# An attention and mixture-of-experts layer on one core: the order and the engines of its first stage changed

## The chip, the core and the metric

The kernel runs on one core of a Trainium2 chip. The metric is the device time of one execution, in microseconds; lower is better. The engines are named PE (TensorE, matrix products), ACT (ScalarE), DVE (VectorE), POOL (GpSimd) and SP (SyncE, which here only issues transfers). ACT and POOL issue transfers as well.

## The reference

Eight batches of 512 tokens with 256 channels. Each batch is normalised, and both an attention with 16 heads and an expert layer read the normalised rows; the output is the input plus both.

```python
xn = _layernorm(x)                                   # (8, 512, 256)
latent = xn @ w_kv_down                              # 256 -> 128
k, v = split(latent @ w_kv_up)                       # 16 heads of 64
q = xn @ w_q
att = softmax(where(causal, q @ k.T / 8, -inf))
y = (att @ v).reshape(..., 1024) @ w_out
logits = xn @ gate_w.T + lb_bias                     # 8 experts, the best 2 of each token
out = x + y + routed_experts(xn, logits) + shared_expert(xn)
```

## The kernel before

Products that need more than one pass's precision are made from a high and a low part: ACT copies a value to the high part (L861), DVE or POOL subtracts it from the value to get the low part (L1138 on DVE, L1350, L1355 and L1403 on POOL), and PE adds three products, high by high, high by low and low by high (L670 to L672). This holds for the weights (`split_w`: parts d, kA, qA, vA for the first heads, and qB, kB, vB for the later ones), the transposed rows, the latent, the queries and the keys.

One list of ticks (`work_order`) sets the order on all five engines. Each engine walks the list and picks what is its own, some of it with a lag in ticks (`LAG`). Engines run apart and meet at semaphores; inside an engine nothing overtakes. The list is built from pairs of heads: pair P stands at 4 P units, and other work is placed at a number of units (`at(u, ...)`, constants in `AT`). Before unit 0 lies the first batch's head: `norm_stats`, `norm_scale`, `norm_rows` (the transposes, L784), `latent`, `query` 0 and `key` 0.

For a pair, PE makes the scores (L693), DVE adds the mask and takes the row maximum (L1242; called the maxima below), ACT exponentiates (L925), PE transposes (L703), ACT or DVE copies the transposed rows (L861, L1248), and PE makes the products with the values (`attend`, L712). The scores of a pair wait for the low part of its query (L1138) and of its key (L1224), both on DVE.

The normalisation of batches 1 to 7 runs beside the first pairs, since routing to experts needs the logits of all tokens. For batch b: `norm_stats` on DVE (L1148, L1154), the reciprocal deviation on POOL (L1342, L1347), `norm_scale` on DVE (L1159), `norm_rows` on PE, ACT and DVE, `gate_logits` and `gate_columns`. Rows live in one of two buffers (`x_in(b)`): x of batch b + 2 can be loaded only after the scaled rows of batch b were stored to `xn_scratch` (L564) and transposed (L568 is the load). The transposed rows go to `xs_scratch` (L571), and the weights of the experts are split one by one (`split_moe`: load L559, ACT, POOL L1355, store L591) and loaded again into `wr` once all rows of batch 7 have been stored (L625). All these transfers are issued by SP, in the order of the ticks.

## Time and profile before

| | |
|---|---|
| time of 3 runs, median (lowest to highest) | 992.47 us (992.27 to 993.35) |
| the profiled execution's own time | 992.81 us |
| its span in the trace | 991.0 us |
| PE busy | 947.4 us (96%) |
| DVE, ACT, POOL busy | 699.7 us (71%), 650.9 us (66%), 350.6 us (35%) |
| mean granted clock of PE | 0.988 |

The span runs from the first to the last instruction. A busy share is an average over stages; the stage that the change touches is the first 125 us of 991. The granted clock is a share of full speed: 1.00 is 2.4 GHz and 0.50 is 1.2 GHz.

### The profile page before, as it was taken

The page shows a single profiled execution, that of the slowest core. Times are in us where ns is not written, and L with a number is a line of the kernel's source. Part 1 is how long each engine was busy: PE and PEld are TensorE (multiplying, and loading weights), DVE is VectorE, ACT ScalarE, POOL GpSimd, SP SyncE. Part 2 cuts the span into 40 slices and gives each one's busy share as a digit, 9 for nine tenths or more (in the row PEclk, how much of TensorE's full clock was granted, in tenths as well). Part 3 has the DMA queues.
Part 4 walks back from the last instruction along what each step waited for, and adds up shares of the span by engine and source line. Part 5 has one row for each costly group of instructions (what it writes and reads, how often), then busy time and mean ns, then how long its engine had stood idle before and what let it go on. Part 6 is the DMA issues. An engine that isn't in the chain of part 4 may idle for free.

```text
span 991.0 us, 20111 instructions
## 1 busy us (share of the span) xinstructions
PE 947.4 (96%) x7136; PEld 758.3 (77%) x7136; DVE 699.7 (71%) x2000; ACT 650.9 (66%) x1801; POOL 350.6 (35%) x349
## 2 busy tenths in 40 slices
PE   5679998889999999999999999999999999999998
PEld 4456776667788787888888888888878778777776
DVE  5779699786766657666575656666566786888884
ACT  3747667566767667676666766677666775677772
POOL 0231113453243253532434433444221444444441
PEclk9799999899999999999999999999999999999999
DMA  6486423553234435455354552547434442533421
GB/s 194 160 313 245 163 101 120 170 192 97 86 105 162 140 113 169 123 186 181 95 173 117 203 181 86 165 134 182 160 116 127 154 128 76 179 107 106 123 86 43
DMA packets 66002, 142.76 MB, mean 144 GB/s; under 512 B 7856, under 2 KB 40880, under 8 KB 64112
## 3 DMA queue, kind: packets, MB, share of 16 engines
q1 hardware_dynamic: 52896, 91.77, 28.3%
q0 software_dynamic: 12432, 49.29, 16.1%
q8 instruction: 57, 0.93, 0.4%
q10 hardware_dynamic: 576, 0.42, 0.1%
q14 instruction: 41, 0.34, 0.1%
HBM read 104.76 MB, written 36.70 MB: 143 GB/s over the span
## 4 chain that ended last, share of the span: by engine, by line
PE 84%; issue 7%; DVE 5%; POOL 2%; DMA 1%; ACT 1%; SPq 0%; DVEq 0%; POOLq 0%
PE PS L670 15%; PE PS L671 14%; PE PS L672 14%; PE PS L712 13%; PE PS L703 13%; PE PS L693 12%; PE PS L820 2%; POOL hh L1355 1%; DVE acc L986 1%; DVE pp L1242 1%; DMA xs<-xs_scratch 1%; PE PS L718 1%; POOL rstd L1347 1%; DMA xr<-in_w_moe 0%; DVE acc L1159 0%
## 5 line engine op out<-in xcount | busy, mean ns | idle before, releaser
L925 ACT ACTIVATE pp<-pp,nmax 128x128 f32<-128x128 f32 (+3 forms) x512 | 280.7, 551 | 97.4 <-DVE nmax L1242 97.4
L1242 DVE CUSTOM_DVE_ANT_0 pp<-PS,maskw 128x128 f32<-128x128 f32 (+3 forms) x512 | 215.2, 483 | 4.8 <-PE PS L693 3.4
L1403 POOL TENSOR_TENSOR yy<-yf,yy 128x512 fp32r<-128x512 f32 x63 | 82.4, 1307 | 278.9 <-ACT yy L861 278.5
L703 PE MATMUL PS<-ident,pp 128*128 128x128 f32 x1280 | 165.3, 276 | 0.1
L693 PE MATMUL PS<-qk 64*128 64x256 f32 (+2 forms) x1536 | 146.8, 337 | 15.3 <-issue 8.4
L703 PEld LDWEIGHTS PS<-ident,pp 128*128 128x128 f32 x1280 | 141.1, 140 | 14.9 <-issue 9.9
L712 PE MATMUL PS<-pt,vv 128*64 128x512 f32 (+3 forms) x1024 | 152.0, 439 | 0.0
L693 PEld LDWEIGHTS PS<-qk 64*128 64x128 f32 x1536 | 114.5, 191 | 31.0 <-issue 17.1
L712 PEld LDWEIGHTS PS<-pt,vv 128*64 128x64 f32 x1024 | 67.9, 136 | 90.3 <-issue 74.1
L861 ACT ACTIVATE pt<-PS 128x384 f32<-128x384 f32 (+1 forms) x215 | 108.5, 512 | 3.1 <-PE PS L703 3.1
L1248 DVE COPY pt<-PS 128x384 f32<-128x384 f32 x169 | 99.1, 591 | 12.7 <-PE PS L703 12.7
L1397 POOL TENSOR_TENSOR hh<-hf,hh 128x256 fp32r<-128x256 f32 (+1 forms) x55 | 49.6, 901 | 147.1 <-ACT hh L861 146.3
L925 ACT ACTIVATION_READ_ACCUMULATOR pp<-pp,nmax 128x1 f32 x512 | 96.4, 188 | 0.0
L1379 POOL DMA_INDIRECT xr<-xn_scratch,lg x78 | 74.5, 955 | 33.5 <-issue 13.8
L670 PE MATMUL PS<-woH,yy 128*128 128x256 f32 x256 | 78.5, 307 | 3.4 <-DVE acc L1209 1.9
L861 ACT ACTIVATE yy<-yf 128x512 fp32r<-128x512 f32 (+1 forms) x65 | 40.3, 622 | 52.1 <-DVE yf L1260 46.4
L672 PE MATMUL PS<-woH,yy 128*128 128x256 f32 x256 | 72.8, 284 | 0.0
L671 PE MATMUL PS<-woL,yy 128*128 128x256 f32 x256 | 72.8, 284 | 0.0
L1260 DVE TENSOR_TENSOR yf<-PS,rb 128x512 f32<-128x512 f32 x63 | 43.4, 689 | 41.2 <-PE PS L712 41.2
L1224 DVE SCALAR_TENSOR_TENSOR qk<-PS,qk 128x512 fp32r<-128x512 f32 x64 | 44.0, 688 | 35.3 <-ACT qk L910 35.0
L1390 POOL DMA_INDIRECT xg<-y_scratch,lg x64 | 61.8, 966 | 18.1 <-issue 14.7
L1138 DVE TENSOR_TENSOR qk<-PS,qk 128x512 fp32r<-128x512 f32 x64 | 44.1, 688 | 28.2 <-ACT qk L861 27.4
(166 smaller groups left out, 2051.7 us busy)
## 6 DMA issues: line engine op xcount, KB each, us to landing
rb<-rr_scratch SPq DMA_DIRECT2D x128, 128.0 KB
wr<-wm_scratch SPq DMA_DIRECT2D x16, 768.0 KB, 5.4
y_scratch<-acc SPq DMA_DIRECT2D x39, 256.0 KB
acc<-in_x SPq DMA_DIRECT2D x15, 512.0 KB, 5.4
wm_scratch<-hh SPq DMA_DIRECT2D x10, 768.0 KB, 4.0
xs_scratch<-wr SPq DMA_DIRECT2D x7, 1024.0 KB, 5.3
xs<-xs_scratch SPq DMA_DIRECT2D x7, 1024.0 KB, 4.7
xn_scratch<-acc SPq DMA_DIRECT2D x8, 512.0 KB, 3.1
```

Of the source, the lines that this page charges most:

```text
L670: e.matmul(o, aH, bH, start=first and i == 0, stop=False)
L671: e.matmul(o, aH, bL, start=False, stop=False)
L672: done = e.matmul(o, aL, bH, start=False, stop=last and i == len(pairs) - 1)
L693: done = e.matmul(bank(kind, i, 2 * j + h)[:, at:at + n], a[r, q], m[r, 0:n], start=first is True, stop=first is None)
L703: done = e.transpose(o, pp[:, i % 4, P_AT[t] + 128 * kt:P_AT[t] + 128 * kt + 128], ident[:, :])
L712: done = e.matmul(g[64 * h:64 * h + 64, 128 * kt:512], vv[:, i // 2 % 2, kt, n % 4, :], pt[:, n % 4, PT_AT[kt]:PT_AT[kt] + 512 - 128 * kt] ...
L861: return e.activation(o, i, ACT.Copy)
L925: e.activation(scores, scores, ACT.Exp, scale=-1.0, bias=nmax[:, b, t:t + 1], accum_out=rs[:, i % 4, 2 * t + h:2 * t + h + 1]).then_inc(a_ ...
L1242: e.tensor_tensor_reduce(pp[:, b, P_AT[t]:P_AT[t] + n], g[:, at:at + n], maskw[:, 512 - n:512], -1.0, 3e38, ALU.add, ALU.min, accum_out=nm ...
L1248: e.tensor_copy(pt_part(i, j), bank(kind, i, j)[:, 0:512 if j == 0 else 384]).then_inc(v_pt, 1)
L1379: e.indirect_dma_start(xr[:, 2 * (b % 2) + t, :], None, xn_d[:, :], bass.IndirectOffsetOnAxis(token_of[:, n:n + 1], 0)).then_inc(d_xr[b % ...
L1403: e.tensor_tensor(yy[:, i % 2, 1, :], yf[:, :], f32(yy[:, i % 2, 0, :]), ALU.subtract).then_inc(g_yl, 1)
```

## The change

TensorE multiplies a tile of ones by itself 15 times before the first transposes and 5 times before the first latent, into a bank that is overwritten. The first batch's x is issued half by SP and half by ACT, and transfers that are needed later are issued later. `query` 1 is placed before the scores of pair 0, `key` 1 and `query` 2 soon after them. The low parts of qB, kB and vB are computed by POOL and no longer by DVE, and they signal `g_wlo` where they signalled `v_wlo`. The mask's first 384 columns, which are zero, are set by POOL, and 128 columns are loaded. `norm_stats`, `norm_scale` and `norm_rows` of batches 1 to 7 are placed 0.6 to 0.8 units later, and the first two `split_moe` 4.3 units later.

```diff
@@ constants
-AT = {"query": (0.0, 0.9), "key": (2.3, 2.0), "value": (1.1, 2.1), "out_part": (3.2, 0.2), "stats": -3.7,
-      "scale": -2.2, "rows": -1.6, "first": 54.0, "last": 176.0, "split": -1.3, "experts": 23.0, "shared0": 17.0,
+AT = {"query": (0.0, 0.9), "key": (2.3, 2.0), "value": (1.1, 2.1), "out_part": (3.2, 0.2), "stats": -3.1,
+      "scale": -1.6, "rows": -0.8, "first": 54.0, "last": 176.0, "split": 3.0, "experts": 23.0, "shared0": 17.0,
@@ def work_order
-        at(4 * (P - 2) + AT["query"][P % 2] if P else -9, "query", P)
-        at(4 * (P - 2) + AT["key"][P % 2] if P else -8, "key", P)
+        at(4 * (P - 2) + AT["query"][P % 2] if P > 2 else (-9, -6, -1.5)[P], "query", P)
+        at(4 * (P - 2) + AT["key"][P % 2] if P > 1 else (-8, -3.5)[P], "key", P)
-    for u, name in ((-8.5, "vA"), (-1.3, "qB"), (-1.2, "kB"), (-1.1, "vB")):
+    for u, name in ((-6.5, "qB"), (-1.2, "kB"), (-1.1, "vB")):
     put("split_w", "kA")
-    put("split_w", "qA")
     for c in range(2):
         put("norm_rows", 0, c)
         tick()
+    put("split_w", "qA")
+    put("split_w", "vA")
@@ def sync_program
-            for t in range(4):
+            for t in range(2):
                 e.dma_start(x_in(0)[:, t, :], x[0, 128 * t:128 * t + 128, :]).then_inc(d_x0[t], 16)
-            e.dma_start(ident[:, :], consts[:, 0:128]).then_inc(d_ident, 16)
             for name in WEIGHT_PARTS:
                 e.dma_start(raw_w[name][0], raw_w[name][1]).then_inc(d_wraw[name], 16)
                 if name == "vA":
-                    e.dma_start(x_in(1), rows128(x[1])).then_inc(d_xin[1], 16)
+                    e.dma_start(hf[:, 0, 0:128], consts[:, 1184:1312]).then_inc(d_mask, 16)
+            e.dma_start(x_in(1), rows128(x[1])).then_inc(d_xin[1], 16)
+            e.dma_start(lb[:, :], lb_bias).then_inc(d_lb, 16)
+            e.dma_start(kc[:, :], consts[:, 384:672]).then_inc(d_kc, 16)
@@ def tensor_program
+            def warm(n):
+                for _ in range(n):
+                    e.matmul(bank("latent", 0, 0)[:, 0:128], ones[:, :], ones[:, :], start=True, stop=True)
+            w.wait_ge(g_cst, 1)
+            warm(15)
...
                 elif kind == "latent":
+                    if not i:
+                        warm(5)
@@ def scalar_program
-            e.dma_start(gw[:, :, :], gate_w).then_inc(d_gw, 16)
-            e.dma_start(hf[:, 0, :], consts[:, 800:1312]).then_inc(d_mask, 16)
-            e.dma_start(lb[:, :], lb_bias).then_inc(d_lb, 16)
-            e.dma_start(kc[:, :], consts[:, 384:672]).then_inc(d_kc, 16)
+            for t in range(2, 4):
+                e.dma_start(x_in(0)[:, t, :], x[0, 128 * t:128 * t + 128, :]).then_inc(d_x0[t], 16)
+            e.dma_start(ident[:, :], consts[:, 0:128]).then_inc(d_ident, 16)
+            e.dma_start(gw[:, :, :], gate_w).then_inc(d_gw, 16)
@@ def vector_program
-                elif kind == "split_w" and lag == 0:
+                elif kind == "split_w" and lag == 0 and i not in LATE_PARTS:
@@ def gpsimd_program
+            e.memset(maskw[:, 0:384], 0.0).then_inc(g_cst, 1)
+                elif kind == "split_w" and lag == 0 and i in LATE_PARTS:
+                    raw, _, oH, oL = raw_w[i]
+                    w.wait_ge(a_whi, whi_at[i])
+                    e.tensor_tensor(oL, raw, f32(oH), ALU.subtract).then_inc(g_wlo, 1)
```

`LATE_PARTS` is qB, kB and vB. All waits on their low parts (three on PE, one on DVE, two on SP) now ask for `g_wlo`.

Three places of the order carry the prediction. The first is DVE's list between the maxima of pair 0 and those of pair 1, before the change; `qk<-PS,qk` at L1138 is the low part of query 1, and at L1224 that of key 1.

```order
L1138 TENSOR_TENSOR qk<-PS,qk 128x512 [waits s_a_q]
L1148 BN_STATS st<-acc 128x6 [waits s_d_xin1,s_v_mv]
L1148 BN_STATS st<-acc 128x6 x3
L1154 BN_AGGR mv<-st 128x2 [waits s_v_st,s_g_ve,s_v_xn]
L1154 BN_AGGR mv<-st 128x2 [waits s_v_st] x3
L1138 TENSOR_TENSOR wqL<-pp,wqH 128x2x768 [waits s_a_whi]
L1138 TENSOR_TENSOR wkL<-acc,wkH 128x768 [waits s_a_whi]
L1138 TENSOR_TENSOR wvL<-xr,wvH 128x768 [waits s_a_whi]
L1224 SCALAR_TENSOR_TENSOR qk<-PS,qk 128x512 [waits s_a_k]
L1159 TENSOR_SCALAR acc<-acc,mv,rstd 128x256 [waits s_g_rstd]
L1159 TENSOR_SCALAR acc<-acc,mv,rstd 128x256 x3
L1253 RECIPROCAL rr<-rs 128x8 [waits s_a_exp]
```

The same place of DVE's list in the changed kernel, from the last of the maxima of pair 0 to the first of pair 1 (lines are those of the changed file); the query here is number 2.

```order
L1241 SCALAR_TENSOR_TENSOR qk<-PS,qk 128x512 [waits s_a_k]
L1155 TENSOR_TENSOR qk<-PS,qk 128x512 [waits s_a_q]
L1165 BN_STATS st<-acc 128x6 [waits s_d_xin1,s_v_mv]
L1165 BN_STATS st<-acc 128x6 x3
L1171 BN_AGGR mv<-st 128x2 [waits s_v_st,s_g_ve,s_v_xn]
L1171 BN_AGGR mv<-st 128x2 [waits s_v_st] x3
L1271 RECIPROCAL rr<-rs 128x8 [waits s_a_exp]
L1260 ISA pp,nmax<-PS,maskw 128x128 [waits s_g_wlo,s_p_S]
```

The low part of key 1 now comes first and nothing of the weights is left on DVE; the low part of query 2 stands ahead of the statistics, and the scaling of batch 1 (L1159 before) is gone from here. It stands behind the maxima of pair 1, in front of the next part of DVE's list:

```order
L1176 TENSOR_SCALAR acc<-acc,mv,rstd 128x256 [waits s_g_rstd]
L1176 TENSOR_SCALAR acc<-acc,mv,rstd 128x256 x3
L1165 BN_STATS st<-acc 128x6 [waits s_d_xin0,s_v_mv]
L1165 BN_STATS st<-acc 128x6 x3
L1171 BN_AGGR mv<-st 128x2 [waits s_v_st,s_g_ve,s_v_xn]
L1171 BN_AGGR mv<-st 128x2 [waits s_v_st] x3
L1266 COPY pt<-PS 128x384 [waits s_p_T]
L1155 TENSOR_TENSOR wr<-PS,wr 128x512 [waits s_a_xth] x2
L1196 TENSOR_TENSOR lg<-PS,lb 128x32 [waits s_d_lb,s_p_lgc]
L1176 TENSOR_SCALAR acc<-acc,mv,rstd 128x256 [waits s_g_rstd]
L1176 TENSOR_SCALAR acc<-acc,mv,rstd 128x256 x3
L1165 BN_STATS st<-acc 128x6 [waits s_d_xin1,s_v_mv]
```

Both scalings (of batches 1 and 2) are followed by statistics, and the last row, the statistics of batch 3, waits for a load of x that SP issues. SP's list around that load, before the change, from the store of batch 1's rows (L564) to the load (L568):

```order
L564 DMA xn_scratch<-acc 128x4x256 [waits s_v_xn]
L591 DMA wm_scratch<-hh 128x1536 [waits s_g_wm]
L559 DMA xr<-in_w_moe 128x768
L659 DMA acc<-in_w_out 128x1024
L568 DMA acc<-in_x 128x4x256 [waits s_d_xn1,s_p_xt]
```

And in the changed kernel, from the same store (L572) to the same load (L576):

```order
L572 DMA xn_scratch<-acc 128x4x256 [waits s_v_xn]
L604 DMA rr_scratch<-rrT 4x2x128 [waits s_a_rb]
L579 DMA xs_scratch<-wr 128x2048 [waits s_v_xtl]
L612 DMA rb<-rr_scratch 64x512 [waits s_v_wlo,s_d_rr]
L612 DMA rb<-rr_scratch 64x512
L576 DMA acc<-in_x 128x4x256 [waits s_d_xn1,s_p_xt]
```

The expert weights and `w_out` are no longer between the two; the reciprocals of pair 0 and the transposed rows of batch 1 (1 MB, waiting for `v_xtl`, DVE's low parts) are.

## Rows read from the trace of the kernel before

**Rows 1.** The page: busy time, share of the span and instructions of PE.

```profile
PE 947.4 (96%) x7136; PEld 758.3 (77%) x7136; DVE 699.7 (71%) x2000; ACT 650.9 (66%) x1801; POOL 350.6 (35%) x349
```

**Rows 2.** Windows: stretch, length, busy time of each engine, granted clock, DMA share, GB/s.

```profile
25.00:50.00 25.00, 15.96 (x94) 11.88 (x95) 18.89 (x61) 18.23 (x43) 7.46 (x9) 0.80 0.51 166
50.00:90.00 40.00, 34.19 (x242) 23.60 (x241) 33.97 (x109) 22.84 (x61) 12.30 (x13) 1.00 0.84 295
90.00:110.00 20.00, 19.84 (x149) 14.40 (x150) 13.63 (x49) 13.02 (x39) 1.29 (x1) 1.00 0.58 217
```

**Rows 3.** Timeline of PE: start, duration, instruction, idle before and its releaser.

```profile
12.14 0.79 PE L670 MATMUL PS<-xs,wdH 128*128 128x512 f32 x1 [1.41 <-DVE xs L1138]
...
19.68 2.20 PE L693 MATMUL PS<-qk 64*128 64x256 f32 x24 [0.34 <-DVE qk L1224]
...
33.26 3.89 PE L693 MATMUL PS<-qk 64*128 64x256 f32 x24 [8.40 <-issue]
```

**Rows 4.** Window 29 to 39 us, columns as in rows 2.

```profile
29.00:39.00 10.00, 5.74 (x29) 4.67 (x30) 8.96 (x25) 4.10 (x12) 1.83 (x1) 0.50 0.31 94
```

**Rows 5.** Timeline of DVE, 5 to 86 us.

```profile
5.26 0.94 DVE L1148 BATCH_NORM_STATS2 st<-acc 128x6 f32<-128x256 f32 x2 [0.42 <-DMA acc<-in_x]
...
10.02 0.69 DVE L1138 TENSOR_TENSOR wqL<-pp,wqH 128x512 fp32r<-128x512 f32 x1 [0.34 <-ACT wqH L861]
...
20.77 0.29 DVE L1242 CUSTOM_DVE_ANT_0 pp<-PS,maskw 128x128 f32<-128x128 f32 x1 [1.23 <-issue]
...
29.06 1.76 DVE L1138 TENSOR_TENSOR wqL<-pp,wqH 128x1536 fp32r<-128x1536 f32 x1 [2.65 <-ACT wqH L861]
...
32.48 0.68 DVE L1224 SCALAR_TENSOR_TENSOR qk<-PS,qk 128x512 fp32r<-128x512 f32 x1
...
34.91 0.29 DVE L1242 CUSTOM_DVE_ANT_0 pp<-PS,maskw 128x128 f32<-128x128 f32 x1 [0.35 <-PE PS L693]
...
46.89 1.41 DVE L1148 BATCH_NORM_STATS2 st<-acc 128x6 f32<-128x256 f32 x4 [0.43 <-DMA acc<-in_x]
...
50.86 2.65 DVE L1159 TENSOR_SCALAR acc<-acc,mv,rstd 128x256 f32<-128x256 f32 x4
...
59.97 1.40 DVE L1148 BATCH_NORM_STATS2 st<-acc 128x6 f32<-128x256 f32 x4 [2.55 <-DMA acc<-in_x]
...
85.02 1.41 DVE L1148 BATCH_NORM_STATS2 st<-acc 128x6 f32<-128x256 f32 x4
```

**Rows 6.** Timeline of ACT, the split of qB.

```profile
27.56 1.48 ACT L861 ACTIVATE wqH<-pp 128x1536 fp32r<-128x1536 f32 x1
```

**Rows 7.** Timeline of SP's issues, batches 1 and 3: store, then next load.

```profile
34.48 0.37 SPq L564 DMA_DIRECT2D xn_scratch<-acc  x1
...
40.58 0.38 SPq L568 DMA_DIRECT2D acc<-in_x  x1
...
55.16 0.51 SPq L564 DMA_DIRECT2D xn_scratch<-acc  x1
...
61.31 0.38 SPq L568 DMA_DIRECT2D acc<-in_x  x1
```

**Rows 8.** The loads of x at L568 before 110 us, from issue to landing.

```profile
DMA to landing us min/median/max: 3.9/5.3/7.6
```

**Rows 9.** Timeline of POOL, a split of 768 columns and one of 1024.

```profile
36.62 1.83 POOL L1355 TENSOR_TENSOR hh<-xr,hh 128x768 fp32r<-128x768 f32 x1 [8.75 <-ACT hh L861]
...
49.99 2.40 POOL L1350 TENSOR_TENSOR woL<-acc,woH 128x1024 fp32r<-128x1024 f32 x1
```

**Rows 10.** Timeline of PE: the scores of pair 4, and the first expert product.

```profile
89.96 2.21 PE L693 MATMUL PS<-qk 64*128 64x256 f32 x24
...
113.23 0.47 PE L670 MATMUL PS<-xs,wr 128*128 128x512 f32 x1
```

**Rows 11.** Transfers issued from 90 to 115 us: size, median time from issue to landing.

```profile
wr<-wm_scratch SPq DMA_DIRECT2D x3, 768.0 KB, 6.4
xs_scratch<-wr SPq DMA_DIRECT2D x2, 1024.0 KB, 4.6
```

More of the change, by code:

```diff
@@ L40 @@
 WEIGHT_PARTS = ("d", "kA", "qA", "vA", "qB", "kB", "vB")
+LATE_PARTS = WEIGHT_PARTS[4:]
 BUSY_HEADS = range(7, 22)
@@ L341, in attention_moe_kernel @@
             new_sem("v_" + n) for n in ("max", "pt", "rr", "y", "yl", "bt", "sg", "h", "add", "fx"))
-        g_cst, g_ve, g_rstd, g_wm, g_wo, g_yl, g_hl, g_sel = (
-            new_sem("g_" + n) for n in ("cst", "ve", "rstd", "wm", "wo", "yl", "hl", "sel"))
+        g_cst, g_wlo, g_ve, g_rstd, g_wm, g_wo, g_yl, g_hl, g_sel = (
+            new_sem("g_" + n) for n in ("cst", "wlo", "ve", "rstd", "wm", "wo", "yl", "hl", "sel"))
         block = ctx.enter_context(nc.Block())
@@ L369, in attention_moe_kernel, with low_weights @@
         whi_at = {n: i + 1 for i, n in enumerate(WEIGHT_PARTS)}
+        def low_weights(name):
+            return (g_wlo, whi_at[name] - 4) if name in LATE_PARTS else (v_wlo, whi_at[name])
         group_of = {k: item[-1] for k, item in enumerate(items)}
@@ L557, in moe_load @@
                 else:
-                    w.wait_ge(v_wlo, whi_at["vB"])
+                    w.wait_ge(*low_weights("vB"))
                 e.dma_start(xr_w, w_moe[SPLIT_ORDER[q]]).then_inc(d_wmraw, 16)
@@ L657, in sync_program @@
                     else:
-                        w.wait_ge(v_wlo, whi_at["kB"])
+                        w.wait_ge(*low_weights("kB"))
                     e.dma_start(acc[:, 0, :, :].rearrange("p t n -> p (t n)"), out_w(i)[0]).then_inc(d_wout, 16)
@@ L722, in tensor_program @@
                     w.wait_ge(*xs_ready(b))
-                    w.wait_ge(v_wlo, whi_at["qA" if p < 2 else "qB"])
+                    w.wait_ge(*low_weights("qA" if p < 2 else "qB"))
                     w.wait_ge(*free)
@@ L730, in tensor_program @@
                     w.wait_ge(v_lat, b + 1)
-                    w.wait_ge(v_wlo, whi_at["kA" if p < 2 else "kB"])
+                    w.wait_ge(*low_weights("kA" if p < 2 else "kB"))
                     w.wait_ge(*free)
@@ L737, in tensor_program @@
                     w.wait_ge(v_lat, b + 1)
-                    w.wait_ge(v_wlo, whi_at["vB" if g4 else "vA"])
+                    w.wait_ge(*low_weights("vB" if g4 else "vA"))
                     w.wait_ge(*free)
@@ L787, in tensor_program @@
                     w.wait_ge(v_xtl, 2 * i + 2)
-                    w.wait_ge(v_cst, 2)
+                    w.wait_ge(v_cst, 3)
                     w.wait_ge(*free)
@@ L1165, in vector_program @@
                     if i == "vA":
+                        w.wait_ge(d_mask, 16)
+                        e.tensor_copy(maskw[:, 384:512], hf[:, 0, 0:128]).then_inc(v_cst, 1)
                         w.wait_ge(d_gw, 16)
                         e.tensor_copy(gwH[:, :, :], gw[:, :, :]).then_inc(v_cst, 1)
-                        w.wait_ge(v_cst, 1)
+                        w.wait_ge(v_cst, 2)
                         low(gwL[:, :, :], gw[:, :, :], gwH[:, :, :]).then_inc(v_cst, 1)
-                        w.wait_ge(d_mask, 16)
-                        e.tensor_copy(maskw[:, :], hf[:, 0, :]).then_inc(v_cst, 1)
                 elif kind == "norm_rows" and lag == 1:
@@ L1226, in vector_program @@
                 elif kind == "scores" and lag == LAG["max"]:
-                    w.wait_ge(v_cst, 3)
+                    w.wait_ge(v_cst, 1)
+                    w.wait_ge(g_cst, 3)
                     for h in range(2):
@@ L1240, in vector_program @@
                             else:
-                                w.wait_ge(v_wlo, whi_at["qB" if i else "kA"])
+                                w.wait_ge(*low_weights("qB" if i else "kA"))
                             e.tensor_tensor_reduce(pp[:, b, P_AT[t]:P_AT[t] + n], g[:, at:at + n], maskw[:, 512 - n:512], -1.0, 3e38, ALU.add, ALU.min,
```

## The prediction, made before the changed kernel was run

> **What bounds the kernel now.** I read the page first: PE is busy 947.4 us of 991.0 [rows 1], so 43.6 us of idle time is all that an edit without less PE work can win. The windows say where it lies [rows 2]: from 25 to 50 us PE is busy 15.96 of 25 us, from 50 to 90 us 34.19 of 40, from 90 to 110 us 19.84 of 20. From 90 us on PE has no room, and its work there is the same before and after the change. So the question is how much earlier PE reaches the place in its list that it now reaches at 89.96 us, the scores of pair 4 [rows 10]; up to there both kernels have done the same pieces except the warming products.
>
> Up to 90 us PE waits for others. DVE is busy 33.97 of 40 us between 50 and 90, and the transfers 0.84 [rows 2]. The timeline of PE shows the largest wait: 8.40 us before the scores of pair 1 at 33.26, which then take 3.89 us, where the same 24 products took 2.20 at 19.68 [rows 3]. The granted clock is 0.50 from 29 to 39 us [rows 4], the lower of the two levels; PE had stood still since 25. DVE's timeline says what was waited for: the low part of key 1 starts at 32.48, queued behind the splits of qB, kB and vB from 29.06, and those waited 2.65 us for ACT [rows 5]. Later DVE itself waits for x: 0.43 us at 46.89, 2.55 us at 59.97 [rows 5].
>
> **The change part by part.** I follow the chain to four marks.
>
> *To the maxima of pair 0.* DVE's statistics of the last two x tiles start at 5.26 [rows 5]. Two of four tiles now go by ACT's queue, ahead of the constants that used to be there. I take 1.0 us for it; bounds 0 and 1.4 (four statistics of some 0.45 in a row cannot end much before 5). wqL (0.69 us at 10.02) no longer stands before the low parts of x [rows 5]: 0.7. The latent thus starts near 12.14 - 1.7 = 10.4 [rows 3]. Fifteen warming products are 128 columns wide in two passes, which I estimate at 0.43 us each at the lower level (as many column passes as half a latent product, at two cycles a column), so they end by 7.4 at the latest, when the transposes start; the five others fill the gap before the latent (1.1 us at the higher level, 2.1 at the lower). If the clock is then at 2.4 GHz, the latent and query 0 save up to 1.6 us: by the ratio of the two scores, 3.89 to 2.20 [rows 3], on the 3.6 us that they take before the clock rises now. Scores 0 could start at 16 to 17 instead of 19.68, with query 1 (1.4 us) already done. But DVE has the low part of query 1 ahead of the maxima, and ACT makes its high part only after the split of qB, 1.48 us [rows 6]: value copy to 15.7, split to 17.2, query copy 0.6, low part 0.7. Maxima of pair 0 start at 18.4, against 20.77 [rows 5]: 2.4 earlier.
>
> *To the maxima of pair 1.* They take 3.4 us; key 1's low part follows (0.68) and PE starts scores 1 at 22.5 instead of 33.26 [rows 3]. The 8.40 us wait is gone and the 1.7 us of slow clock too, as no idle time is left that is near the one before 29 us. What is late next is DVE: it waits for query 2's high part on ACT. ACT's list up to the split of qB reaches 27.56, which is 6.8 us after the maxima began at 20.77 [rows 5, 6]; the new list up to query 2 has the same pieces, so 25.2. Then 0.7 low part, 1.75 statistics: the maxima of pair 1 start at 27.6 instead of 34.91 [rows 5]: 7.3 earlier.
>
> *To the load of x for batch 3.* The scaling of batch 1 now stands behind these maxima, and its deviation is computed on POOL behind three splits. POOL takes 1.83 us for 768 columns [rows 9]: qB's 1536 from 17.2 to 20.9, kB and vB to 29.7, then 1.4 for the deviation: 31.1. The maxima end at 31.0. The scaling ends at 32.5, its store is issued there instead of at 34.48 [rows 7]: only 2.0 earlier. Five of the 7.3 us are handed back. The load of batch 3 was issued 6.1 us after the store and landed 6.3 us later (40.58, then DVE at 46.89) [rows 5, 7]. Now SP must first issue the 1 MB of transposed rows, which wait for statistics 2, a copy and two low parts on DVE (32.5 + 3.8 = 36.3), and two broadcasts: load at 38.0, landed after 5.3 to 6.3 [rows 7, 8], 43.8. DVE stands idle from 37.9 on, some 6 us. Batch 3's statistics: 3.1 earlier, and the low part of key 2 with the scores of pair 2 behind them.
>
> *To the scores of pair 4.* From 43.8: statistics and key 2 2.4, copies and low parts 2.6, maxima of pair 2 3.4, scaling 1.4: batch 3's store at 53.6 (before: 55.16). Its load comes 6.15 later, as 61.31 came after 55.16 [rows 7], and lands 5.3 later [rows 8]: 65.1. Statistics 1.7, 2.5 of copies, maxima 3.4, low part 0.6, scaling 1.4: 74.7; store to load 4.0, landing 5.3: batch 7's statistics at 84.0 instead of 85.02 [rows 5]. Key 4's low part now follows them at once (2.4 us), and PE's transposes of batch 6 are done by then: scores of pair 4 at 86.4 instead of 89.96 [rows 10], 3.6 earlier. Bounds: 84.1 if x is never late (PE's own list), 88.5 if each of three loads lands 0.7 us later.
>
> *Behind it.* The rows of batch 7 are transposed ten ticks' worth of work later, in front of the first expert product (23.3 us after the scores of pair 4, at 113.23) [rows 10]. Their store can be issued 13.7 after the scores, lands in 4.6, and then the weights load, 5.0 to 6.4 [rows 11]: 23.3 to 24.7. I take a new wait of 0.5 us.
>
> Costs of nothing: the mask and the memset (POOL idle, 0.3 us of DVE saved); the later splits of the first experts (ACT 0.84, POOL 1.83 [rows 9]; they leave the crowded stretch, are due only for the weight loads behind the norms, and cost nothing as long as they end by then); gate weights early.
>
> Sum: 3.6 - 0.5 = 3.1 us off 992.81, the profiled execution's own time: 989.7. The median of the runs is 0.34 lower, so 989.4.
>
> Two rules of the Trainium skill bear on this. The DMA page (DMA: Bandwidth & Descriptors, Issuing engines are not separate DMA queues) says that transfers from several engines run on the same 16 DMA engines, so that two queues save only issue time; by it the x term would be the time of two issues, about 0.9 us, and no trace here shows x issued that way yet. The GPSIMD page (GPSIMD Engine Reference, Key points) says that GpSimd shares its SBUF interfaces with VectorE, which speaks against moving the splits to POOL. The trace agrees in one place: four scalings beside POOL's split at 49.99 took 2.65 us [rows 5, 9], about twice what they take alone. By that rule, if it hit one or two groups of four on the chain to the load of x, the sum would be 1.3 to 2.6 us worse; without it, it stays 3.1.
>
> **The rivals.**
> A: x is not what limits. If the loads land in 3.9 [rows 8] and stores clear quickly, DVE's idle 6 us near 40 and the waits behind it shrink, and the 7.3 us of the second mark mostly stays. For it: DVE loses 3.7 us of work. Against it: the same load already ended two waits of DVE [rows 5]. Gain 5 to 7.5, time 986.0.
> B: all is handed back. The chain store, load, statistics, maxima, scaling takes 38.1 us for two rounds now (46.89 to 85.02 [rows 5]) and 40.2 in my sum, since the maxima stand inside it; if each round loses 0.5 to 1.5 us more, batch 7's statistics stay at 85 to 86.5 and scores 4 at 88.5 to 89: gain 0.4 to 1, time 991.9.
> C, slower: PE waits for the first expert weights. The store of batch 7's rows and the weight load need 4.6 + 6.4 us behind a start 13.7 to 15 us after scores 4; with landings as long as 7.6 [rows 8] that is 29 us against 23.3, a wait of up to 5.7. It decides the sign once that wait exceeds the gain at scores 4. Time 994.6.
> D: the warming does not raise the clock, or it falls back before the latent. Then PE enters the latent at the lower level and the five products delay it by 1 us: the first mark is 1 to 2.6 us worse, of which ACT's split hides about half. Time 990.6. The forecast of the clock rests on PE having worked at the lower level from 12.14 and from 33.26 for less than 6 us each time before its products were fast [rows 3, 4]; 15 products at that level last 6.4.
>
> **How the numbers follow.** Likeliest 0.45 (989.4, own range 988 to 991.2), A 0.25, B 0.18, C 0.06, D 0.06. A measurement of this kernel tells about 0.2%, 2 us, from no change: faster means below 990.5. Faster: 0.85 of the likeliest, all of A, a third of D: 0.65; slower 0.06, the rest 0.29. The range reaches from A's middle to B: 985.8 to 992.2, which leaves out half of A's tail and C.
>
> **What would show it.** In the changed trace: warming products until 5 to 7.4 us and the latent's six products done in 1.4 us; maxima of pair 0 at 18.4, scores 1 at 22.5, no window at 0.50 between 25 and 45; maxima of pair 1 near 27.6; DVE waiting some 6 us for x before statistics 3 near 43.8; scores 4 at 86.4; a PE wait below 1 us before the first expert product. I am wrong if DVE does not wait for x near 40 (A), if statistics 7 are not earlier than 85 (B), or if a wait for `wr` of over 2 us stands near 110 (C).

## The result and the profile after

| | before | changed |
|---|---|---|
| median of the runs | 992.61 us (991.65 to 993.35, 6 runs) | 997.50 us (994.31 to 998.14, 6 runs) |
| ratio to before, 95% interval | 1 | 1.0044, 1.0030 to 1.0058 |
| profiled execution, span | 992.81 us, 991.0 us | 994.31 us, 992.5 us |
| PE busy | 947.4 us | 954.5 us |

The changed kernel is 0.4% slower; two more measurements gave 1.0051 and 1.0056. The forecast, 989.4 with a range from 985.8 to 992.2 us, does not hold it. The profiled execution is the quickest of its six. One execution, of e9 below, is left out of its ratio: it took 1323 us at a mean granted clock of 0.66, where its eleven others took 1004.5 to 1011.1.

The page's line of busy times; of PE's 7.1 us more than in [rows 1], 6.12 are the first fifteen unused products, shown below. So the 10 us more that PE is busy up to 50 us, in the windows that follow, are not 10 us of progress:

```profile
PE 954.5 (96%) x7176; PEld 764.0 (77%) x7176; DVE 693.1 (70%) x1997; ACT 651.7 (66%) x1801; POOL 358.4 (36%) x353
```

The windows of [rows 2], of after. Up to 50 us PE does 39.65 us of work where it did 29.63; from 50 to 110 it does 50.27 where it did 54.03:

```profile
0.00:25.00 25.00, 22.49 (x138) 18.35 (x138) 13.22 (x43) 14.25 (x33) 5.57 (x10) 1.00 0.60 185
25.00:50.00 25.00, 17.16 (x91) 11.53 (x92) 17.96 (x72) 14.47 (x39) 10.56 (x10) 0.74 0.55 175
50.00:90.00 40.00, 31.95 (x208) 21.85 (x206) 25.14 (x84) 22.60 (x57) 11.45 (x11) 0.95 0.84 296
90.00:110.00 20.00, 18.32 (x130) 13.78 (x132) 14.08 (x45) 11.13 (x30) 2.54 (x3) 0.91 0.36 132
```

PE's timeline (start, duration, engine, line, operation, operands, count, and in brackets the idle time before it and what ended it). The wait of 8.40 us before the scores of pair 1 [rows 3] is gone; two new ones stand before the scores of pair 2 (4.22) and of pair 4 (5.30), and the scores behind both take 3.89 and 3.46 us instead of 2.19:

```profile
0.98 6.12 PE L686 MATMUL PS<-ones 128*128 128x128 f32 x30 [0.98 <-POOL half L1354]
7.59 1.64 PE L801 MATMUL PS<-ident,acc 128*128 128x128 f32 x8 [0.49 <-DVE acc L1176]
...
10.80 0.50 PE L678 MATMUL PS<-xs,wdH 128*128 128x512 f32 x1 [0.46 <-DVE xs L1155]
...
22.79 2.19 PE L708 MATMUL PS<-qk 64*128 64x256 f32 x24
...
46.03 3.89 PE L708 MATMUL PS<-qk 64*128 64x256 f32 x24 [4.22 <-DVE qk L1241]
...
67.51 2.80 PE L708 MATMUL PS<-qk 64*128 64x384 f32 x12 [2.40 <-DVE pt L1266]
...
91.68 0.56 PE L812 MATMUL PS<-ident,hf 8*128 8x8 f32 x4 [5.30 <-DVE qk L1241]
92.19 3.46 PE L708 MATMUL PS<-qk 64*128 64x256 f32 x24
```

DVE's timeline, against [rows 5]: maxima of pair 0 (18.69) and of pair 1 (27.26), scaling 1, and the statistics of batches 3, 5 and 7, each behind a wait for x:

```profile
18.69 0.28 DVE L1260 CUSTOM_DVE_ANT_0 pp<-PS,maskw 128x128 f32<-128x128 f32 x1
...
27.26 0.24 DVE L1260 CUSTOM_DVE_ANT_0 pp<-PS,maskw 128x128 f32<-128x128 f32 x1
...
30.73 1.38 DVE L1176 TENSOR_SCALAR acc<-acc,mv,rstd 128x256 f32<-128x256 f32 x4 [0.15 <-POOL rstd L1366]
...
43.72 1.41 DVE L1165 BATCH_NORM_STATS2 st<-acc 128x6 f32<-128x256 f32 x4 [6.57 <-DMA acc<-in_x]
...
65.19 1.41 DVE L1165 BATCH_NORM_STATS2 st<-acc 128x6 f32<-128x256 f32 x4 [2.92 <-DMA acc<-in_x]
...
73.55 1.37 DVE L1176 TENSOR_SCALAR acc<-acc,mv,rstd 128x256 f32<-128x256 f32 x4
...
89.27 1.41 DVE L1165 BATCH_NORM_STATS2 st<-acc 128x6 f32<-128x256 f32 x4 [6.51 <-DMA acc<-in_x]
```

SP's timeline, first behind batch 1's scaling, then behind batch 5's. The store of the normalised x (`xn_scratch<-acc`) and the load of the x that takes its place (`acc<-in_x`, 38.27 and 83.82) are 6.1 and 8.9 us apart. Between them stand the store of the row reciprocals, the 1 MB store of transposed rows (`xs_scratch<-wr`), which waits for DVE's low parts, and two broadcasts. Behind 74.95 SP waits 3.4 us for ACT's copy of the reciprocals and 2.0 us for the low parts:

```profile
32.15 0.37 SPq L572 DMA_DIRECT2D xn_scratch<-acc  x1
...
38.27 0.54 SPq L576 DMA_DIRECT2D acc<-in_x  x1
...
74.95 0.37 SPq L572 DMA_DIRECT2D xn_scratch<-acc  x1
78.75 0.65 SPq L604 DMA_DIRECT2D rr_scratch<-rrT  x1
81.40 0.33 SPq L579 DMA_DIRECT2D xs_scratch<-wr  x1
81.84 1.88 SPq L612 DMA_DIRECT2D rb<-rr_scratch  x2
83.82 0.54 SPq L576 DMA_DIRECT2D acc<-in_x  x1
```

Windows ahead of, in and behind the two new waits (third number from the right: the granted clock). It is 1.00 up to 32 us, and 0.50, the lower of the two levels, from 34 to 40, where PE works most of the time but its products of 512 columns take 0.63 us instead of 0.39. Back at 1.00 from 42, it falls to 0.50 again while PE stands still, and stays there for the scores:

```profile
34.00:40.00 6.00, 4.75 (x16) 2.49 (x15) 2.83 (x8) 2.82 (x5) 1.07 (x2) 0.50 0.67 224
44.00:46.00 2.00, 0.00 (x0) 0.00 (x0) 2.00 (x10) 0.07 (x1) 0.42 (x2) 0.50 0.51 200
46.00:50.00 4.00, 3.96 (x25) 3.17 (x26) 4.00 (x17) 2.13 (x8) 4.00 (x3) 0.50 0.46 135
92.00:95.00 3.00, 3.00 (x23) 2.89 (x24) 3.00 (x10) 0.20 (x1) 0.40 (x1) 0.50 0.02 5
```

### The profile page after: what moved, and what is told of

Same layout as the page of the kernel before. It is cut to its first block, busy times and chain, and to the rows that moved or that the text cites. A ratio compares the mean times of both kernels' runs of the same rounds, so it can differ in the third digit from the quotient of the medians.

```text
span 992.5 us, 20191 instructions
## 1 busy us (share of the span) xinstructions
PE 954.5 (96%) x7176; PEld 764.0 (77%) x7176; DVE 693.1 (70%) x1997; ACT 651.7 (66%) x1801; POOL 358.4 (36%) x353
## 4 chain that ended last, share of the span: by engine, by line
PE 84%; DVE 5%; issue 4%; DMA 3%; POOL 2%; ACT 1%; SPq 1%; DVEq 0%; POOLq 0%; ACTq 0%
PE PS L678 15%; PE PS L679 14%; PE PS L680 14%; PE PS L727 13%; PE PS L718 13%; PE PS L708 12%; PE PS L837 2%; DMA xn_scratch<-acc 1%; DMA acc<-in_x 1%; DVE acc L1003 1%; DVE pp L1260 1%; PE PS L733 1%; DMA xs<-xs_scratch 1%; POOL hh L1378 1%; DMA xr<-in_w_moe 0%
```

## The experiments

The experiments ran on four chips. On two (3 and 13) the kernel before takes 992 to 993 us, on the other two (6 and 15) 1010 to 1011; so each ratio is to the kernel before on the same chip, and the last section tells what differs. Runs with the same figure under "kernel before" from e1 on were timed side by side (e1 to e4, e5 to e8, e9 to e12, e13 to e16); a comparison across these groups is weaker. Two columns come from each profiled execution: the start of batch 7's statistics on DVE and of the scores of pair 4 on PE.

| run | ratio, 95% interval | kernel before | stat. 7 | scores 4 |
|---|---|---|---|---|
| before | 1 | 992.6 | 85.02 | 89.96 |
| changed | 1.0044, 1.0030-1.0058 | 992.6 | 89.27 | 92.19 |
| e7, changed again | 1.0051, 1.0039-1.0063 | 992.7 | 90.99 | 93.90 |
| e15, changed, third | 1.0056, 1.0042-1.0069 | 991.6 | 89.57 | 92.48 |
| e1, load ahead | 0.9975, 0.9957-0.9993 | 1010.3 | 82.85 | 86.81 |
| e14, load ahead again | 0.9969, 0.9960-0.9979 | 991.6 | 82.69 | 85.59 |
| e2, norms back | 0.9949, 0.9932-0.9965 | 1010.3 | 79.80 | 86.03 |
| e6, both | 0.9940, 0.9927-0.9954 | 992.7 | 78.23 | 83.19 |
| e8, later norms alone | 1.0201, 1.0188-1.0214 | 992.7 | 104.55 | 107.46 |
| e3, head alone | 0.9981, 0.9969-0.9993 | 1010.3 | 81.08 | 86.07 |
| e4, not warmed | 1.0102, 1.0082-1.0122 | 1010.3 | 92.76 | 95.67 |
| e16, not warmed again | 1.0092, 1.0077-1.0107 | 991.6 | 92.83 | 95.74 |
| e9, both, not warmed | 0.9965, 0.9951-0.9979 | 1011.1 | 81.07 | 85.75 |
| e11, both, experts early | 0.9977, 0.9968-0.9987 | 1011.1 | 85.27 | 90.25 |
| e12, both, one queue | 0.9953, 0.9940-0.9966 | 1011.1 | 78.31 | 83.25 |
| e5, products at the waits | 1.0134, 1.0119-1.0150 | 992.7 | 93.63 | 103.06 |
| e10, the same, other banks | 1.0140, 1.0118-1.0161 | 1011.1 | 93.65 | 103.49 |
| e13, products in the waits | 1.0068, 1.0054-1.0082 | 991.6 | 93.08 | 95.99 |

**Theory 1:** the loads of x come late, because on SP's list the store of the low parts and the broadcasts stand ahead of them, and because later norms start every round of the chain later. **Theory 2:** the loss is the clock that falls in the new waits. **Rival:** the unused products, the second queue or the low parts on POOL do harm themselves. The low parts on POOL and the new places of the queries and keys were not taken out alone.

**The load moved alone, e1 and e14.** In the changed kernel's list of SP:

```diff
-                elif kind == "norm_rows" and lag == 4 and j and i + 2 < NBATCH:
+                elif kind == "norm_rows" and lag == 2 and j and i + 2 < NBATCH:
```

> The changed kernel with one thing moved: on SP's list the x load of a batch stands right behind the store of the batch before it in its buffer, ahead of the rows store, the store of the low parts (which waits for VectorE) and the row broadcasts. Theory 1 (the order of SP's list hands the gain back): batch 5's store at 75.0 is followed by the load of batch 7 as soon as the store has landed, 6.1 us later, at 81.1 and not 83.8; it lands at 86.5; batch 7's statistics start at 86.6 (changed kernel 89.3), scores of pair 4 at 89.5 (92.2): 2.7 off the median of 997.5, 994.8. Theory 2 (not the time of the wait but TensorE's clock falling in it): the scores of pairs 2 and 4 keep 3.9 and 3.5 us as long as a wait stands ahead of them, and the gain is no more than the wait is shorter. Rival (the placement of norms on VectorE is what binds): the load is earlier but statistics 7 are not, 997.5. A price to watch: the rows store and broadcasts go up to 5 us later, which shows as a new wait at the values of y if anything hangs on them.

> The changed kernel with the x load right behind the store on SP's list, beside the changed kernel itself. Theory 1 (the load behind the store of the low parts is the step that failed): 0.006 to 0.008 below the changed kernel's ratio, near the 0.9966 that my sum had. If the chip made the difference in the first call: 0.000 to 0.003 below it.

Measured: 0.9975, and 0.9969 where the changed kernel beside it is at 1.0056: medians of 988.37 and 997.16 us, 8.8 us for one line of SP's program. That is more than the 2.7 us that I had expected for e1, since the load goes ahead in every round: statistics 3, 5 and 7 start 4.7, 3.0 and 6.9 us earlier than in e15. SP's timeline of e14 behind batch 5's scaling; the load goes 5.9 us after the store, and ahead of the rest:

```profile
72.77 0.37 SPq L572 DMA_DIRECT2D xn_scratch<-acc  x1
78.69 0.37 SPq L576 DMA_DIRECT2D acc<-in_x  x1
79.10 0.65 SPq L604 DMA_DIRECT2D rr_scratch<-rrT  x1
```

DVE's and PE's timelines of e14. The wait for x before statistics 3 is 1.93 us (6.57 in the changed kernel), before statistics 7 1.75 (6.51), and PE's wait for key 4 is 0.52 (5.30):

```profile
39.06 1.40 DVE L1165 BATCH_NORM_STATS2 st<-acc 128x6 f32<-128x256 f32 x4 [1.93 <-DMA acc<-in_x]
...
82.69 1.40 DVE L1165 BATCH_NORM_STATS2 st<-acc 128x6 f32<-128x256 f32 x4 [1.75 <-DMA acc<-in_x]
```

```profile
85.09 0.38 PE L812 MATMUL PS<-ident,hf 8*128 8x8 f32 x4 [0.52 <-DVE qk L1241]
```

Issues from 25 to 96 us (KB each, median us from issue to landing), of the changed kernel and of e14. The load lands in 3.9 instead of 5.4 us where it does not go out right behind the 1 MB store:

```profile
acc<-in_x SPq DMA_DIRECT2D x6, 512.0 KB, 5.4
```

```profile
acc<-in_x SPq DMA_DIRECT2D x6, 512.0 KB, 3.9
```

So a round of this chain, batch 5's store to batch 7's statistics, costs 14.3 us in the changed kernel (74.95 to 89.27) and 9.9 in e14 (72.77 to 82.69). The price that I watched for, the later rows store and broadcasts, shows once: PE waits 1.17 us at 53.23 for DVE's copy of y (`yf`), which it does not in the changed kernel. The load does not cure everything: PE still waits 3.08 us at 64.44, and the granted clock is 0.50 from 64 to 70.

**The norms moved alone, e2, and both, e6.**

```diff
-      "scale": -1.6, "rows": -0.8, ...
+      "scale": -2.2, "rows": -1.6, ...
```

with `"stats"` back from -3.1 to -3.7.

> The changed kernel with the three numbers of the norms put back as before (statistics -3.7, scaling -2.2, transposes -1.6 instead of -3.1, -1.6, -0.8). Theory 1 (later norms make stores and x loads late): scaling of batch 1 and its store go before the maxima of pair 1, so the x load of batch 3 is at or ahead of 38, and batches 5 and 7 are 2 to 5 us earlier than in the changed kernel; the waits of 4.2 us before the scores of pair 2 and of 5.3 before pair 4 shrink to 1 or less each; 997.5 less 5 to 8, so 989.5 to 992.5. Against it the scores of pair 1 wait again for VectorE, up to 3 us of it (the maxima of pair 1 are then behind the statistics): so 990 to 994. Rival (the norms' place is not the cause; warming, queues or low parts on POOL are): within 1 of the changed kernel, 996.5 to 998.5.

> The changed kernel with both the norms' three numbers as before and the x load right behind the store on SP's list. With the norms put back alone the kernel was at 0.9949 of the kernel before, with the load moved alone at 0.9975. Theory 1: the chain store to load to statistics has slack once the norms are early, so the second edit adds little: 0.993 to 0.996. If the two parts of the wait add up, 0.990 to 0.992. Rival (the load, waiting for its store's landing on SP, delays the rows store and the row broadcasts, which with early norms are the next in need): 0.996 to 1.000, with PE waiting for the values of y.

Measured: 0.9949 and 0.9940. Either edit takes nearly all of the two waits away; together they give little more than the norms alone (the two intervals overlap, on different chips), since the first already frees the chain. From 25 to 125 us DVE waits for x 16.2 us in the changed kernel, 7.9 in e14, 4.7 in e2 and not at all in e6, and the scores of pairs 2, 3 and 4 all run at the higher clock (PE's timeline of e6):

```profile
42.07 2.21 PE L708 MATMUL PS<-qk 64*128 64x256 f32 x24
...
83.19 2.21 PE L708 MATMUL PS<-qk 64*128 64x256 f32 x24
```

With 986.24 us (984.14 to 987.50) against 992.69 beside it, e6 beats both kernels.

The early norms have a price of their own. In e6 the scaling of batch 1 stands beside POOL's splits of kB and vB and takes 4.42 us, against 1.38 in the changed kernel, where it stands behind them. DVE's and POOL's timelines of e6:

```profile
26.20 4.42 DVE L1176 TENSOR_SCALAR acc<-acc,mv,rstd 128x256 f32<-128x256 f32 x4
```

```profile
26.21 1.80 POOL L1370 TENSOR_TENSOR wkL<-acc,wkH 128x768 fp32r<-128x768 f32 x1
27.97 1.85 POOL L1370 TENSOR_TENSOR wvL<-xr,wvH 128x768 fp32r<-128x768 f32 x1
```

e2, e11 and e12, which also have early norms and POOL's low parts, have 4.42, 4.43 and 4.42 there. So later norms keep this scaling clear of POOL, and that saves DVE 3.0 us; what the later stores and loads cost is more.

**Later norms in the kernel before, e8.** The three numbers of the norms alone, -3.1, -1.6 and -0.8, without any other part.

> The kernel before with one part of the change alone: the three numbers of the norms (statistics -3.1, scaling -1.6, transposes -0.8). Theory 1 (this part is what costs): the maxima of pair 1 start a little earlier, but the stores of batches 1, 3 and 5 and the loads behind them are later; a new wait of 4 to 5 us ahead of the scores of pairs 2 and 4, less what the scores of pair 1 gain; 1.004 to 1.009 of the kernel before. Rival (later norms cost only together with the other parts, since without low parts on POOL the scores of pair 1 end the same wait of 8.4 us): 0.999 to 1.002.

Measured: 1.0201, four times the changed kernel's loss and outside what either theory gave. Without the early low parts the maxima of pair 1 still come late (scores 1 at 35.49), and the scaling of batch 1, now behind them, starts at 42.75 instead of 33.08. Its store goes at 44.15, and the load of batch 3 only at 55.40, behind the store and load of expert weights and the 1 MB store. SP's, DVE's and PE's timelines of e8:

```profile
44.15 0.38 SPq L564 DMA_DIRECT2D xn_scratch<-acc  x1
...
55.40 0.53 SPq L568 DMA_DIRECT2D acc<-in_x  x1
```

```profile
60.93 1.41 DVE L1148 BATCH_NORM_STATS2 st<-acc 128x6 f32<-128x256 f32 x4 [10.35 <-DMA acc<-in_x]
```

```profile
63.25 3.04 PE L693 MATMUL PS<-qk 64*128 64x256 f32 x20 [10.14 <-DVE qk L1224]
```

Later norms are only bearable where the maxima ahead of them are early, and here 11.3 us pass between store and load. **The experts' number put back in e6, e11** (`"split": 3.0` to `-1.3`), shows what their weights do on that list:

> The version with early norms and the early x load, with the number of the first expert splits back at -1.3 (3.0 in it). Then the expert weights' load, their split and its store stand on SP's list between the stores of batches 1, 2 and 3. If stores and loads of x ride on SP's list (theory 1), the store of batch 1 stands behind a load that waits for xr and the store of batch 2 behind the split's store: the x loads of batches 3 and 4 are 2 to 6 us later, 0.996 to 1.001. Rival (the placement of the splits is free, since the wait for the first expert product is none): 0.993 to 0.995.

Measured: 0.9977. The store of batch 1 goes at 31.78, as soon as its scaling is done, but the load of batch 3 only at 38.88, 7.1 us behind it (3.4 in e6): between them stand the store of split expert weights, which goes at 36.98 when POOL's split is done, and the loads of the next ones and of `w_out`. DVE waits 4.94 us for x before statistics 3, and the scores of pair 4 start at 90.25 instead of 83.19. That part of the change is one that pays (side by side, 0.9977 against 0.9953 for e12 and 0.9965 for e9), by taking expert weights out from between store and load of x.

**The products and the queue: e3, e4, e16, e9, e12.** e3 is the kernel before with the products and with x on two queues alone; e4 and e16 are the changed kernel, e9 is e6, all three without the unused products (first diff); e12 is e6 with all four x tiles and the identity issued by SP and none by ACT (second diff).

```diff
-            warm(15)
-                    if not i:
-                        warm(5)
```

```diff
-            for t in range(2):
+            for t in range(4):
                 e.dma_start(x_in(0)[:, t, :], x[0, 128 * t:128 * t + 128, :]).then_inc(d_x0[t], 16)
+            e.dma_start(ident[:, :], consts[:, 0:128]).then_inc(d_ident, 16)
```

> The kernel before with only two parts of the change: the 15 and 5 unused products and x of batch 0 over two queues. Nothing else is moved. Both theories: the latent part starts about 1.7 earlier (10.4 and 10.8 against 12.1), the maxima of pair 0 at 18.5 to 19; the wait of 8.4 us before the scores of pair 1 stays, since it ends with low parts of weights whose raw values still land at the same time: it takes back 1 to 1.7, so the kernel is at 991.3 to 992.6 against 992.6. Rival (the products or the second queue do harm by themselves, by delaying weight loads on the queues or by drawing the clock down later): 994 or more.

> The changed kernel without its 20 unused products. Theories 1 and 2 (the loss sits after 40 us): the transposes of batch 0 and the latent part run at the lower clock, the latent part starts 0.3 to 0.6 later and lasts longer, pair 0 is 1 to 1.5 later; of it the wait before the scores of pair 2 takes back a part; 997.5 to 999. Rival (the unused products bring a later fall of the clock, or a slower mode of the whole run): the kernel comes out faster, 993 to 996, and the granted clock from 43 to 51 us and from 91 to 96 us is no longer at 0.50.

> The changed kernel without its 20 unused products, beside it. By the version with early norms and early load (0.9965 without, 0.9940 with them, on two chips) 0.002 to 0.003 above the changed kernel; by my sum's step (transposes 2.2 and not 1.65, latent part 1.4 and not 0.5 behind them) 0.0015; by the two ratios so far (1.0102 and 1.0051) 0.005.

> The version with early norms and the early x load (0.9940 of the kernel before) without its 20 unused products. If warming is worth what the head shows (transposes 2.2 and not 1.65 us, latent part 1.41 and not 0.46 us behind it: the scores of pair 4 some 1.5 later), 0.9950 to 0.9960. If it is worth the 5 us that the changed kernel seemed to lose with its products (1.0102 against 1.0051, on different chips), 0.999 or so. Rival (warming is worth nothing here, since x and the weights set the head): 0.994.

> The version with early norms and the early x load, with x of batch 0 and the identity issued by SP alone, as before. My first sum gave the second queue 1.0 us (bounds 0 and 1.4): then the transposes of batch 0 start 1.0 later and all behind them, 0.9950. If the head is bound by the weights' landing and not by x, 0.9940; if issue time is all that the second queue saves (two issues of 0.06 us each in the rows), 0.9940 too.

Measured: without the products the changed kernel loses 3.7 us more (medians 1000.86 and 997.16, 1.0092 against 1.0056 side by side). In the version with both edits their worth in time is not clear: e9 stands 0.0025 above e6, from another chip, and 0.0012 above e12 beside it, both with overlapping intervals, though its scores of pair 4 start 2.5 us later (85.75 against 83.25). PE's timeline of e16: the transposes take 2.20 us instead of 1.64, the latent starts behind a wait of 1.41 instead of 0.46, and its products take 0.63 us instead of 0.39. The windows give a granted clock of 1.00 for the head with and without the unused products, so the level there is read from these times:

```profile
7.57 2.20 PE L798 MATMUL PS<-ident,acc 128*128 128x128 f32 x8 [7.57 <-DVE acc L1173]
11.19 0.80 PE L678 MATMUL PS<-xs,wdH 128*128 128x512 f32 x1 [1.41 <-DVE xs L1152]
```

The scores of pair 0 are then 2.0 us later (18.80 against e15's 16.79) and those of pair 4 3.3 (95.74 against 92.48). The growth lies on SP's list between the store of batch 3's rows and the load of batch 5: 8.7 us (54.85 to 63.57) instead of 7.2 (53.16 to 60.41), since SP waits 4.2 instead of 3.2 us for ACT's copy of the reciprocals and 2.6 instead of 2.1 for the store's landing. e4 gave 1.0102 on a slower chip, where the changed kernel itself was not timed. The rival that the products do harm falls, and so does my bound of 2.6 us on their worth. e3 keeps more of its gain than I had written (the wait of 8.40 us before the scores of pair 1 stays, but all stands 2.35 us earlier). In e12 the scores of pair 4 start at 83.25 against 83.19, and the transposes of batch 0 at 7.56 against 8.05: in the traces the second queue gives nothing. The ratios, 0.9953 and 0.9940 from two chips, overlap in their intervals and cannot exclude the 1.0 us. One issue of x takes 0.46 us in e12's rows (four in 1.84), not the 0.06 that I had written.

**Products against the falling clock: e5, e10, e13.** In the changed kernel, with KEEP naming a bank that is free and a count of unused products:

```diff
+                if (kind, i, j) in KEEP:
+                    taker, n = KEEP[kind, i, j]
+                    w.wait_ge(*released(*taker))
+                    for _ in range(n):
+                        e.matmul(bank(*taker)[:, 0:128], ones[:, :], ones[:, :], start=True, stop=True)
```

```diff
+KEEP = {("scores", 2, 0): (("scores", 2, 1), 18), ("gate_columns", 5, 0): (("scores", 4, 0), 22)}
```

That is e13. e10 names `("scores", 2, 2)` and `("scores", 4, 1)` for the banks; e5 has 16 products ahead of the scores (2, 0) and (4, 0), in the bank that they take.

> The changed kernel with 16 more unused products at each of two places, just ahead of the scores of pairs 2 and 4, into the bank that those scores take next. They fill the waits of 4.2 and 5.3 us (about 0.1 to 0.2 us each, so 1.8 to 3.3 us of work at each place) and move nothing else. Theory 1 (what is lost is the x load's lateness): VectorE's statistics 3 and 7 start when they did; the scores of pairs 2 and 4 may run 2.2 us and not 3.9 and 3.5, which is 1.7 and 1.3 back at most: 994.5 to 997.5 on a chip where the changed kernel has 997.5. Theory 2 (the clock's fall is the larger part of the loss, and of the runs near 998): the slow ones of the changed kernel's two kinds of runs go, 993 to 995. Rival (the products end after the wait and push the scores back): 0 to 2 slower than the changed kernel.

> The changed kernel with unused products inside its two waits: 18 ahead of the scores of pair 2, into a bank released since 30 us, and 22 ahead of the gate columns that wait with pair 4, into a bank released since 85 us; so, unlike the first try, they run while PE waits and not behind the wait. Theory 2 (the clock's fall adds to the loss): the scores of pairs 2 and 4 take 2.2 and not 3.9 us, 3.4 less, and the stretch at 68 that makes some runs of the changed kernel near 998 goes too: 1.0000 to 1.0025 against the 1.0051 of the changed kernel. Theory 1 alone (only the time of the wait counts): 1.004 to 1.006. In both, statistics 3 and 7 start no more than 1 earlier than in the changed kernel. Rival (products overrun the wait): above 1.006.

> As e10, but the 18 and 22 unused products go into banks that ScalarE releases at 39 and 84 us in the changed kernel's trace, before the waits begin, so they run from 41.8 and 86.4 on. Theory 2 (the clock's fall is part of the loss): the scores of pairs 2 and 4 take 2.2 each instead of 3.9 and 3.5 to 3.9, the clock stays at 1.00 in both waits: 3 us less than the changed kernel of this call, a ratio 0.003 lower. Theory 1 alone: the same as the changed kernel within 0.001. Rival (products overrun or delay VectorE's key): higher than the changed kernel.

e5 and e10 missed: their banks are released only when the wait ends, so 16 to 22 products ran behind it, in 6.0 to 6.9 us each time, and 1.0134 and 1.0140 are what such work costs on the path. In e13 they ran inside the waits. Windows of e13:

```profile
46.00:48.00 2.00, 0.50 (x6) 0.51 (x8) 2.00 (x9) 0.69 (x1) 0.96 (x2) 0.97 0.15 50
48.00:50.00 2.00, 2.00 (x18) 1.95 (x16) 2.00 (x9) 0.15 (x1) 2.00 (x2) 0.50 0.64 223
94.00:96.00 2.00, 0.42 (x6) 0.33 (x6) 2.00 (x9) 0.00 (x0) 1.06 (x2) 1.00 0.00 0
```

In the second wait the clock stayed at 1.00 and the scores of pair 4 ran at the higher level; in the first it fell to 0.50 at 48 all the same, behind 3.5 us without work (43.98 to 47.50). But DVE's waits for x were longer, 7.94 and 7.73 us, with the load's issue as early (38.37) or 2.1 us later (86.42) than in e15, and its landing 6.7 to 6.8 us after it instead of 5.3 to 5.6:

```profile
45.18 1.41 DVE L1171 BATCH_NORM_STATS2 st<-acc 128x6 f32<-128x256 f32 x4 [7.94 <-DMA acc<-in_x]
...
93.08 1.41 DVE L1171 BATCH_NORM_STATS2 st<-acc 128x6 f32<-128x256 f32 x4 [7.73 <-DMA acc<-in_x]
```

Measured 1.0068, against 1.0056 for the changed kernel beside it, intervals overlapping: theory 2's 0.003 did not come. The clock is a cost, seen in the rows (3.89 and 3.46 us instead of 2.19), and at the second wait holding it up gave 1.4 us back: from the scores of pair 4 to those of pair 5 e13 takes 16.5 us (95.99 to 112.47) and e15 17.9 (92.48 to 110.36). The later landings had put pair 4 off by 3.5 us, so the net was nothing, and what the clock alone is worth is not cleanly shown. With the load or the norms early the slow scores are gone from both places by themselves.

## Why the prediction was wrong, step by step

- *To the maxima of pair 0:* 18.69 for 18.4. Right in sum, with one term put to the wrong cause. The last statistics of batch 0 did end 0.94 us earlier (5.26 instead of 6.20), which is the 1.0 us that I had priced for x on two queues; but in e12, with one queue, they end at 5.14, and in e3, with two queues and ACT still issuing the mask, `lb` and `kc` behind them, at 5.70. That points to these constants, which the change issues later; it was not tested alone. By the page of the Trainium skill (DMA: Bandwidth & Descriptors, Issuing engines are not separate DMA queues) the second queue would have saved only its issue time, about 0.9; here even that did not show.
- *To the maxima of pair 1:* scores 1 at 22.79 for 22.5, maxima at 27.26 for 27.6. Right in the times. The sign "no window at 0.50 between 25 and 45" failed: the granted clock was 0.50 from 34 to 40, behind 10 us (24 to 34) in which PE was busy 7.6. That stretch lay off the chain: PE had caught up and waited from 41.8, for a DVE that had waited for x since 37.15.
- *To the load of x for batch 3:* scaling ends at 32.1 for 32.5, load at 38.27 for 38.0, landed 43.7 for 43.8. Right, the order of SP's list included.
- *To the scores of pair 4:* here it failed. Batch 5's statistics, 65.19 for 65.1, and scaling, done at 74.9 for 74.7, still hold, the first with some luck: batch 3's store was 0.5 us earlier than forecast (53.11), the load 7.4 and not 6.15 behind it, and the landing took 4.7 and not 5.3. The step "store to load 4.0, landing 5.3" was 8.9 and 5.4. I had read SP's list for batch 3, and for batch 7, where the same four instructions stand ahead of the load, I took the time of a store's landing alone. It is also too short for that: with nothing ahead, e14 has 5.9, of which SP waits 5.5 for the store to land. Statistics 7 were at 89.27 for 84.0, scores 4 at 92.19 for 86.4. With the load ahead, e14 has 82.69 and 85.59, and 0.9969 of 992.6 is 989.5 us. That this meets the forecast is in part luck, since e14 is earlier at pair 4 than the forecast and has a stretch at 0.50 (64 to 70 us) that the forecast had not. This was rival B's mechanism: the two rounds from statistics 3 to statistics 7 took 45.55 us, against 40.2 in my sum. I had allowed 0.5 to 1.5 us more a round; its place and sign were seen, its size was not.
- *The clock:* I let it stay up in the wait that I had forecast myself. The scores of pairs 2 and 4 took 1.7 and 1.25 us more, and a stretch at 0.50 near 68 comes on top. A stretch at 0.66 from 225 to 230 stands in e7's profile (span 996.8) and not in the first one (992.5). It is a part of what lies between the two: e7 is 2.6 us later at the scores of pair 5 (112.05 and 109.41) and 4.2 later at one copy of ACT behind the stretch (255.43 and 251.24). Windows of e7 and of the first:

```profile
225.00:230.00 5.00, 5.00 (x32) 4.27 (x32) 2.37 (x7) 1.60 (x4) 1.94 (x2) 0.66 0.16 56
```

```profile
225.00:230.00 5.00, 5.00 (x47) 4.31 (x46) 4.74 (x22) 4.42 (x15) 0.00 (x0) 1.00 0.02 5
```

- *Behind it:* no wait before the first expert product; rival C is refuted, and my 0.5 us was too much. The store of batch 7's rows goes at 106.47, 14.3 behind the scores, the weights at 111.05, and the product starts at 116.62.
- *Rival D:* the other way round. The products raised the clock, and were worth 3.7 us in the changed kernel and not 1 to 2.6.
- *The rule against POOL,* the Trainium skill's (GPSIMD Engine Reference, Key points) that GpSimd shares its SBUF interfaces with VectorE, did not come into play in the changed kernel. Its seven scalings up to 98 us took 1.37 to 1.38 us each, since none stood beside a split of POOL, but for 0.1 us at 61.6. The other runs bear the rule out: a group of four takes 4.42 us beside two splits in e6, 2.47 beside one in e14 (46.94). That page of the Trainium skill names only some of VectorE's instructions; batch 1's statistics in the changed kernel kept their 1.40 us beside the split of kB.

The failed step in one line: the wait from the store of batch 5's rows to the load of batch 7 was put at 4.0 us and was 8.9, since the load stood on SP's list behind two waiting stores. The cost of it in e15 against e14: the scores of pair 4 start 6.9 us later (92.48 and 85.59), and those of pair 5, behind the slower products, 8.3 (110.36 and 102.07). The two profiled executions end 7.3 us apart and the medians 8.8.

What stays open: why a 512 KB load landed 1.2 to 1.4 us later in e13 than in e15 while PE ran unused products, since in e14 it lands in 4.0 while PE works on the kernel's own; and what each of the untested parts, the low parts on POOL above all, is worth alone.

## What to carry to other kernels

A load that reuses a stored buffer is as late as the list of its issuing queue makes it: read, for every round and not for the first only, what stands between the store and the load, and what each of those waits for. Where the chain store, load, statistics, store has no slack, moving its link later to make room for something else is paid in every round; look first whether the load can be issued ahead of its neighbours. A forecast wait of PE is a reason to expect the lower clock behind it, and in this kernel unused products paid at the start and not as a patch on a wait. Where work goes to POOL, look which of DVE's instructions will stand beside it.

## What the runs showed of the hardware that I had not expected

The kernel before took 992 to 993 us on two chips and 1010 to 1011 on two others, at the same mean granted clock (0.986 to 0.993 and 0.985 to 0.992). In the profiles of the slower chips ACT pauses before its exponentials with nothing in the trace that it waits for, 36.7 us in 11 times in e3, the longest 5.6 us, and 32 to 48 us in the other seven profiles; the other chips' profiles have no such row. DVE pauses too (7.6 us in 5 times in e3). The wait view of e3 (waiting instruction, releaser, us in total, times, longest):

```profile
ACT pp L936 <- issue: 36.7, 11, 5.6
```

In e3 all of ACT's pauses lie behind 110 us, 29.1 of ACT's 36.7 us behind 700, where the work is the same in every kernel, so the comparisons on one chip stand. What the engines pause for is not known.
